# One delta layer of ten cycles in place of eleven fenced stages, its last solve moved into the stage behind it

## What is computed

```python
def step(S, inp):
    qt, kt, vt, at, gkt = inp
    Sp = S * jnp.exp(gkt)[..., None]
    u = jnp.einsum('bhk,bhkv->bhv', at, Sp) + vt
    S = Sp + jnp.einsum('bhk,bhv->bhkv', kt, u)
    o = jnp.einsum('bhk,bhkv->bhv', qt, S)
    return (S, o)
...
out = out.reshape(b, n, d)
gate = jax.nn.sigmoid(x @ Wg1 @ Wg2)
out = out * gate
mu = jnp.mean(out, axis=-1, keepdims=True)
var = jnp.mean(jnp.square(out - mu), axis=-1, keepdims=True)
out = (out - mu) * jax.lax.rsqrt(var + 1e-05) * norm_w
return out @ Wo
```

## Time and profile before

| what | value |
|---|---|
| median of 3 runs | 1835.32 us (1829.82 to 1835.4) |
| the profiled execution | 1837.21 us, span of its core 1835.0 us |
| PE busy | 1648.3 us (90%) |
| DVE busy | 1103.2 us (60%) |
| ACT busy | 688.4 us (38%) |
| POOL busy | 333.8 us (18%) |
| first delta stage starts | 1197 us |
| stage 10 starts | 1650.7 us |
| the stage of the tail starts | 1677.9 us |
| the feed-forward stage starts | 1754.8 us |

### The profile page before, as it was taken

One profiled execution on the slowest core, in us unless ns is written; L12 is line 12 of the kernel. 1 busy time (PEld: TensorE's weight loads), 2 busy tenths in 40 slices (PEclk: granted clock), 3 DMA queues, 4 the chain that ended last, 5 costly groups with the idle time before them and its releaser, 6 DMA issues. The chain is left out here.

```text
span 1835.0 us, 49212 instructions
## 1 busy us (share of the span) xinstructions
PE 1648.3 (90%) x21601; PEld 1476.2 (80%) x21601; DVE 1103.2 (60%) x2417; ACT 688.4 (38%) x1436; POOL 333.8 (18%) x331
## 2 busy tenths in 40 slices
PE   8899968999999999999999999776888888766789
PEld 8788756998889999999999999656877777765668
DVE  7677757555454555546455455557566666653885
ACT  6466644332232222223222232253433434333642
POOL 4633335000000000000000000153222222200830
PEclk9999979999999999999999999876666666655899
DMA  6000011000010000001000000100000000001001
GB/s 212 1 2 3 2 49 46 1 24 24 1 47 1 24 24 24 24 1 47 1 24 24 1 1 1 39 1 2 4 3 4 3 3 4 4 4 52 1 12 44
DMA packets 11701, 36.10 MB, mean 20 GB/s; under 512 B 3400, under 2 KB 8032, under 8 KB 8928
## 3 DMA queue, kind: packets, MB, share of 16 engines
q1 hardware_dynamic: 11488, 32.97, 5.2%
HBM read 30.47 MB, written 2.49 MB: 18 GB/s over the span
## 5 line engine op out<-in xcount | busy, mean ns | idle before, releaser
L1126 ACT ACTIVATE hidden<-bank,moe_b 128x512 f32<-128x512 f32 (+1 forms) x320 | 213.3, 668 | 536.8 <-PE bank L1018 524.2
L1035 PE MATMUL bank<-moe_w2h,hidden_hi 128*128 128x256 f32 x1216 | 345.7, 284 | 0.0
L1035 PE MATMUL bank<-moe_w2l,hidden_hi 128*128 128x256 f32 x1216 | 344.0, 283 | 0.0
L1035 PE MATMUL bank<-moe_w2h,hidden_lo 128*128 128x256 f32 x1216 | 344.0, 283 | 0.0
L1160 DVE SCALAR_TENSOR_TENSOR residual<-bank,gates,residual 128x256 f32<-128x256 f32 x152 | 73.4, 484 | 290.4 <-PE bank L1035 290.4
L1018 PE MATMUL bank<-x_hi,moe_w1h 128*128 128x512 f32 (+1 forms) x640 | 243.8, 381 | 2.8 <-ACT hidden L1126 2.8
L1018 PE MATMUL bank<-x_lo,moe_w1h 128*128 128x512 f32 (+1 forms) x640 | 242.5, 379 | 0.0
L1018 PE MATMUL bank<-x_hi,moe_w1l 128*128 128x512 f32 (+1 forms) x640 | 242.0, 378 | 0.0
L1035 PEld LDWEIGHTS bank<-moe_w2h,hidden_hi 128*128 128x128 f32 x1216 | 233.1, 192 | 6.0 <-DVE residual L1160 4.3
L1035 PEld LDWEIGHTS bank<-moe_w2l,hidden_hi 128*128 128x128 f32 x1216 | 233.2, 192 | 1.2
L1035 PEld LDWEIGHTS bank<-moe_w2h,hidden_lo 128*128 128x128 f32 x1216 | 233.2, 192 | 0.0
(11 more groups left out here) (315 smaller groups left out, 3239.8 us busy)
## 6 DMA issues: line engine op xcount, KB each, us to landing
moe_w<-in_moe_w SPq DMA_DIRECT2D x16, 1024.0 KB, 4.8
patches<-in_patches SPq DMA_DIRECT2D x7, 864.0 KB, 6.3
out<-residual SPq DMA_DIRECT2D x19, 128.0 KB, 1.7
ffn_w<-in_ffn_w SPq DMA_DIRECT2D x2, 1024.0 KB, 5.9
att_w<-in_att_w SPq DMA_DIRECT2D x1, 1536.0 KB, 9.4
delta_w<-in_delta_w SPq DMA_DIRECT2D x1, 1280.0 KB
patches<-in_patches SPq DMA_DIRECT2D x6, 144.0 KB, 2.9
tok_w<-in_tok_w SPq DMA_DIRECT2D x6, 128.0 KB, 2.6
```

The lines of the kernel that those rows point to most:

```text
L1035: mm = nc.tensor.matmul(bank[4 + n % 3][:, 0:D], left, right, start=(i == 0), stop=(i == len(passes) - 1))
L1126: nc.scalar.activation(H[:, i % 4, 0:n], bank[i % 4][:, 0:n], ACT.Relu, bias=b1[:, x, f:f + 1]).then_inc(acted, 1)
```

## The change

`delta_stage` becomes `delta_layer`: one stage, in which each engine's program runs `part(*roles(k))` for k from 0 to 9. There are no barriers inside. Each semaphore counts on over the chunks (a wait for `silu` of n becomes one for 4 * nxt + n, and so on), and waits are added where only the barrier kept order. The order of the instructions on every engine stays as it was. The solve and output of the last chunk (the former stage 10) go into `output_tail`, among the gates. The buffers that this solve reads are now allocated apart, so that they outlive the delta layer; the gates are kept in the tile that then takes the gated output. The tail's banks are numbered anew, the two sums of magnitudes are parted, and the scales are made inside the loop.

```diff
-            for k in range(CHUNKS + 3):
-                delta_stage(nc, psum, bank, b, k - 1 if 1 <= k <= CHUNKS else None, k if k < CHUNKS else None,
-                            k - 2 if 2 <= k < CHUNKS + 2 else None, k - 3 if k >= 3 else None)
+            delta_layer(nc, psum, bank, b, CHUNKS + 2)
...
+    def roles(k):
+
+        return (k - 1 if 1 <= k <= CHUNKS else None, k if k < CHUNKS else None,
+                k - 2 if 2 <= k < CHUNKS + 2 else None, k - 3 if 3 <= k < CHUNKS + 3 else None)
...
+                def project(n):
+                    if n == 0 and nxt >= 1:
+                        pe.wait_ge(k_max, HALVES * nxt)
+                    if n == 0 and z:
+                        pe.wait_ge(t_back, 3 * z)
...
+                def values(p):
+                    if p == 0:
+                        pe.wait_ge(in_hi, HALVES * (c + 1))
+                        pe.wait_ge(in_lo, HALVES * (c + 1))
+                        if c == 0:
+                            pe.wait_ge(g1_lo, len(spans))
+                        else:
+                            pe.wait_ge(d_exp, CB * c)
...
+                def a_rows():
+                    pe.wait_ge(pa_ready, 2 * CB * (z + 1))
+                    pe.wait_ge(scale_ready, z + 1)
...
+                def keys_in_pair(m, e):
+                    if m == 0 and e == 0:
+                        pool.wait_ge(k_unit, HALVES * (c + 1))
+                        if c >= 1:
+                            pool.wait_ge(dscores, IP * c)
...
+            for k in range(stages):
+                part(*roles(k))
```

The tail, on PE:

```diff
-            for t in range(LEAD):
+            def gates_and_rows(t):
                 gate(2 * t)
                 gate(2 * t + 1)
                 token_rows(t)
+
+            first_half(0)
+            gates_and_rows(0)
+            first_half(1)
+            gates_and_rows(1)
+            gates_and_rows(2)
+            remainder(0)
+            gates_and_rows(3)
+            remainder(1)
+            gates_and_rows(4)
+            gates_and_rows(5)
+            second_half(0)
+            gates_and_rows(6)
+            second_half(1)
+            gates_and_rows(7)
+            gates_and_rows(8)
             gate(2 * LEAD)
-            pe.wait_ge(abs_sum, 2)
-            pe.wait_ge(ones_set, 1)
-            nc.tensor.matmul(bank[7][:, 0:2], ones[:, :], S[:, 0, :], start=True, stop=True).then_inc(total, 1)
+            output(0)
+            output(1)
             for j in range(TILES + 3):
                 if j < TILES:
                     turn_gated(j)
                 token_rows(j + LEAD)
                 if 0 <= j - 1 < TILES:
                     project(j - 1)
+                if j == 2:
+                    pe.wait_ge(abs_sum, 2)
+                    pe.wait_ge(ones_set, 1)
+                    pe.wait_ge(o_whole, 2)
+                    nc.tensor.matmul(bank[3][:, 0:2], ones[:, :], S[:, 0, :], start=True, stop=True).then_inc(total, 1)
```

and on DVE:

```diff
+            for t in range(3):
+                measured(t)
+            with_values(0)
+            measured(3)
+            with_values(1)
+            for t in range(4, 7):
+                measured(t)
+            magnitude(0)
+            measured(7)
+            measured(8)
             gated_stats(LEAD - 1)
             gated_aggregate(LEAD - 2)
             gated_aggregate(LEAD - 1)
-            dve.wait_ge(loaded, 64)
+            inverses(0)
             for i in range(2):
-                nc.vector.tensor_reduce(S[:, 0, i:i + 1], flat[i], AX.X, ALU.add,
-                                        apply_absolute_value=True).then_inc(abs_sum, 1)
-            inverses(0)
...
+                whole_out(i, 0)
+                whole_out(i, 1)
+            magnitude(1)
             for j in range(TILES + 5):
                 if 0 <= j - 1 < TILES:
                     low_gated(j - 1)
+                if j == 2:
+                    for i in range(2):
+                        low_out(i, 0)
+                        low_out(i, 1)
+                if j == 3:
+                    scales()
```

More of the change, by code:

```diff
@@ new lines, in remainder @@
+            def remainder(i):
+                pe.wait_ge(u1_back, i + 1)
+                for lane in range(LANES)[lanes(i)]:
+                    for n in range(2):
+                        rows = slice(PAD * n, PAD * n + HB)
+                        mm = nc.tensor.matmul(bank[i][PAD * n + HB:PAD * n + HB + HALF, place(lane)],
+                                              pa_y[rows, lane, 1, HALF:SEQ], RX[rows, lane, :],
+                                              start=True, stop=True)
+                mm.then_inc(r_done, 1)
@@ new lines, in output @@
+            def output(i):
+                pe.wait_ge(u2_back, i + 1)
+                for p in (2 * i, 2 * i + 1):
+                    for m in range(HALVES):
+                        for n in range(2):
+                            for g in range(PPH):
+                                lane = p * HEADS + m * HPH + 2 * g
+                                mm = nc.tensor.matmul(
+                                    own_and_other(i, n)[32 * g:32 * g + 32, m, p % 2], UB[half(n), lane // 2, :],
+                                    pa_y[half(n), lane:lane + 2, 0, :], start=True, stop=True)
+                mm.then_inc(o_done, 1)
@@ L1604, in _, with measured @@
             nc.vector.memset(ones[:], 1.0).then_inc(ones_set, 1)
-            for t in range(LEAD):
+            def measured(t):
                 gated(t)
@@ L2358, in ternary_ffn @@
+                for b in range(2, CB):
+                    steps(b)
+            for k in range(stages):
+                part(*roles(k))
 def ternary_ffn(nc, sb, bank, RES, XH, XL, out, w1t, w2t, b1, b2):
```

1309 lines of the change are left out of this document (718 added, 591 removed), and 1 row of the table UB.

## The result

| | before | after |
|---|---|---|
| median | 1833.42 us (1829.82 to 1835.4, 4 runs) | 1804.35 us (1799.05 to 1806.38, 4 runs) |
| profiled execution, span | 1837.21, 1835.0 us | 1806.38, 1804.6 us |
| granted clock of PE over the span | 0.880 | 0.883 |

The ratio is 0.9839, with a 95% interval from 0.9811 to 0.9868: 29.1 us less by the medians, 30.4 by the spans. The forecast was 24.5 less.

What follows compares the result with a forecast made beforehand. PE's queue was taken to bound full stages, with stage 10 and the tail's head as waiting chains. Layer 14.9 us (11.9 + 0.7 + 3.3 - 1) plus tail 9.6 made 24.5 off 1835.3: 1810.8 us, range 1801 to 1821.

Steps and rivals of the forecast that it cites:

- The seven boundaries: Delta layer: without barriers PE goes from `inverse_out` straight to `a_rows`, 1.7 us gained at each, 11.9 us in all.
- The boundary into cycle 2: Delta layer: PE was idle 2.48 us; `a_rows` now waits only for DVE's last `weigh`, gain 0.7 us.
- The boundary into cycle 1: Delta layer: `values` began after 5.70 us of idleness and will wait only for `g1_lo`, gain 3.3 us.
- The rival of the clock: Delta layer: without idleness ahead, `values` run at 2.4 GHz from their start in eight cycles, 15 us, 1796; chance 0.08.
- The ninth rows at 28.3 us: Tail's head, from its start: PE work 26.3 us, plus 0.5 for instruction stalls and 1.5 for the 2 MB loads.
- From the ninth rows to the first product: Tail: DVE's chain of statistics, root, norm, `whole_out` and second magnitude puts the loop's first product at 38.1 us.
- 1.3 late: Tail's head: the moved-up magnitude holds DVE 2.2 us between tiles 7 and 8, some 0.9 of it in idle time.
- another 1.0: Tail's head: 1.0 us on DVE for the product and statistics of the tile before, still queued.
- The loop: Tail's loop: DVE gets four `low_out` and the scales, covered by its idle time; counted as nothing, -1.5 to +1.5 us.
- the boundaries give back: Rival, delta layer: a 1.4 us stall follows in each `first_half`, the layer gains 5.1 us, 1820.6; chance 0.13.
- slower: Rival: instruction supply sets the pace of the unbroken program, stalls use up the gain, up to 1853; chance 0.03.
- the head doesn't interleave: Rival, tail: loads cost their upper bound and DVE holds up the rows, tail gives 3.0 us, 1817.4; chance 0.12.

Runs made afterwards that it cites:

- tail_alone: The kernel before, its ten stages with barriers kept, given only the new end stage with the last solve: 1824.91 us, ratio 0.9942.
- solve_first: The changed kernel with its head not interleaved, all six pieces of the solve ahead of gates and token rows: 1817.04 us, ratio 0.99.
- cycle1_later: The changed kernel with the first `values` of cycle 1 waiting also for POOL's first key piece: 1812.45 us, ratio 0.9873.

## Why the prediction was right, and where its terms were off

The sign, the size and both mechanisms held: 24.5 us forecast, 29.1 measured, and 1804.35 lies in the range. It was too small because terms were off in both places, nearly all to one side.

- **The seven boundaries, 11.9 us.** 11.5 in this pair of traces, 13.9 on the averages (two traces with barriers, eleven without). Counting all of PE's wait for the barrier was right, and so was that nothing behind it would be late. What I named as the work that the barrier waits for, ACT's `inverse_back`, is 1.0 of the 1.7, by the added wait. The 1 us that I took off for added waits wasn't there. The cycles that I gave 52.6 us took 52.6 to 54.4, by the clock they found.
- **The boundary into cycle 2, 0.7 us.** PE's wait there went from 2.48 to 1.78, for DVE as said.
- **The boundary into cycle 1, 3.3 us.** PE's wait went from 5.70 to 2.46, 3.2, as said: `values` wait for `g1_lo`. The failed step is that I priced a shorter standing still at its own length. PE kept 2.4 GHz across it, and cycle 1's 324 matmuls took 4.2 us less. Cycles 0 and 1 together gave 7.0 where I had 4.0. Part of that is luck: on the averages they give 5.4, as the first stages of `tail_alone` took 44.6 us and not 46.3, and as in three of eleven unbroken layers the clock fell in the 2.46 us all the same.
- **The rival of the clock** (0.08) looked for this effect at eight boundaries, where the clock is at 0.50 before the boundary in any case. There it didn't come: a granted clock of 0.63 in the four-role cycles after, 0.62 to 0.67 before. The place that it missed is the one where PE came to the wait at 2.4 GHz, and there it came in eight of eleven traces.
- **The ninth rows at 28.3 us.** 27.0 in the change, 27.0 to 28.3 in the ten interleaved kernels, 27.8 on average. The terms for instructions (0.5) and for the loads (1.5) together should have been 0.4 to 1.4. The transfer's 1.5 us exists, in a head that isn't interleaved; I charged it where the gates and rows leave the supply of instructions time. By the Trainium skill's rule that such fetches are mostly hidden (Runtime: NRT & Kernel Launch, Instruction fetch mechanics) both would be nothing: true to 0.4 us in the interleaved order, false by 8.1 us in the other.
- **From the ninth rows to the first product, 9.8 us.** 7.2. Two terms failed. "1.3 late" for the magnitude that moved up: it was in a gap that left 0.71 us over; and "another 1.0" for a tile's product and statistics still queued: DVE was idle, and its last statistics ended 1.4 us behind the ninth product's start. The chain from there (table, root, two small ones, `whole_out`, magnitude) took 5.8, and I had 6.2. Together with the head this makes 13.5 where I had 9.6.
- **The loop, 0 with 1.5 either way.** 1.3 lost, inside the bound, but not by what I named. `low_out` cost nothing. POOL's work ended 6.1 us ahead of PE's last turn (1716.6 and 1722.7), as I had said, and my question was the wrong one: not whether POOL is late, but what it does to DVE while it runs.
- **The signs to look for.** The barrier's row gone, `a_rows` at the heel of `inverse_out`, `values` of cycle 1 earlier, the magnitude behind `whole_out` as DVE's last before the loop, POOL done before PE's last turn: all there. Waits for instructions in the layer didn't grow. Of the rivals, "the boundaries give back" and "slower" fall with the 13.9 us and with PE's "issue" waits from cycle 2 to 9 (18.3 before, 14.7 in the change), and "the head doesn't interleave" with the trace of `solve_first`, which is what it would have looked like.

## What to carry to other kernels

A barrier between stages costs what the slowest engine's last piece lies behind the bounding engine, and some 0.7 us of its own. A wait that gets shorter can be worth more than its length where the engine comes to it at the full clock, but not in every run: here the clock stayed up across 2.46 us in eight traces of eleven. Tiny matmuls in a row outrun the supply of their instructions, so put a few long ones between them: here that hid nearly 8 us, and a 2 MB transfer besides. And when an engine becomes free earlier, look for what it runs beside: a one-column DVE instruction of 0.16 us took up to 0.74 beside a POOL instruction with two tensors in SBUF, and 0.17 beside one that reads a single one.

## What the runs showed of the hardware that was not expected

- A DVE instruction with two SBUF operands is held until POOL's instruction with two SBUF operands ends (up to 0.74 us for one column), and the two engines fall into step, so that a loop of 2.34 us a turn runs at 2.70. Beside POOL's instruction with one operand it isn't held (0.16 to 0.19), and the DVE form with a per-partition scalar isn't held by either (0.22).
- 2.46 us without a matmul left PE at 2.4 GHz in eight traces and brought it to 1.2 GHz in three; 5.70 us (twice) and 5.92 us brought it down each time. With 5.70 us before and 5.92 us in `cycle1_later` the level was low for some 6.8 us, of which 6 and 3 lay behind the wait.
- The same seven cycles, with the same instructions in eleven kernels, took 350.7 to 360.4 us, at granted clocks between 0.63 and 0.66: 2.7% of the layer, and 0.5% of the whole time.
- Beside a 2 MB transfer an "issue" wait of PE took 3.00 us, and 0.84 with the transfer moved behind it (one trace each).
